# Layer norm, linear attention and a mixture of experts in one kernel: where the last batch's routed operand is made, and the order of the routing steps

## The reference

```python
xn = _layernorm(x)
s = _L0_attn_ref(xn, ...)             # 16 heads of 8 channels, softmax over 1024 keys, plus a depthwise conv of v
def _experts_mlp(x, g, W1, b1, W2, b2):
    xn = _rmsnorm(x, g)               # x * rsqrt(mean(x*x) + eps) * g
    h = gelu(einsum('btc,ech->bteh', xn, W1) + b1)      # 128 -> 512
    return einsum('bteh,ehc->btec', h, W2) + b2         # 512 -> 128
h_s = _experts_mlp(u, g_shared, ...).sum(axis=-2)       # 2 shared experts, all tokens
scores = sigmoid(u @ centroids)                         # 8 routed experts
gpk, i_topk = top_k(scores, 2)
gk = gpk / scores.sum(axis=-1, keepdims=True)
h_r = sum over the 2 picks of gk * routed expert of that pick
return u + h_s + h_r                                    # u is xn
x = x + s * silu(...)
```

## Time and profile before

| | us |
|---|---|
| device time, median of 3 runs | 1215.17 (1215.11 to 1217.58) |
| the profiled execution | 1215.84 |
| its span | 1213.8 |
| PE busy in the span | 1150.0 (95%) |
| DVE busy | 831.8 (69%) |
| ACT busy | 750.3 (62%) |
| POOL busy | 392.2 (32%) |

### The profile page before, as it was taken

The page is one execution under the profiler, slowest core; times in us unless marked ns, Lnnn a source line. Parts: engine busy times, 40 slices in busy tenths (PEclk is TensorE's granted clock), DMA queues, the critical chain, the costliest instruction groups (busy, mean ns, idle before and its releaser), DMA issues.

```text
span 1213.8 us, 18390 instructions
## 1 busy us (share of the span) xinstructions
PE 1150.0 (95%) x6564; PEld 727.3 (60%) x6564; DVE 831.8 (69%) x1562; ACT 750.3 (62%) x1385; POOL 392.2 (32%) x436
## 2 busy tenths in 40 slices
PE   4899949979998999999999999999999999999996
PEld 3788839979985545555554555555455555545542
DVE  6642213235637888888889888888988888898870
ACT  4544416635546767666676666667666666766676
POOL 0055565020006543514324351432435043243000
PEclk8799979989999999999999999999999999999998
DMA  9011133555433212020211203021111202112000
GB/s 335 5 41 38 42 102 113 165 142 150 141 104 80 55 39 53 20 75 11 58 37 35 52 18 77 11 58 36 35 44 28 75 11 58 37 35 51 9 6 5
DMA packets 73866, 75.36 MB, mean 62 GB/s; under 512 B 25248, under 2 KB 58912, under 8 KB 73264
## 3 DMA queue, kind: packets, MB, share of 16 engines
q1 hardware_dynamic: 69680, 65.80, 19.7%
q0 software_dynamic: 4096, 8.40, 2.4%
HBM read 30.06 MB, written 18.35 MB: 40 GB/s over the span
## 4 chain that ended last, share of the span: by engine, by line
PE 63%; DVE 6%; issue 1%; ACT 0%; POOLq 0%; POOL 0%; DVEq 0%; ACTq 0%
PE ps L1377 22%; PE ps L1389 20%; PE ps L1034 18%; DVE neg_half L1101 4%; PE ps L1055 1%; DVE acc L1448 1%; PE ps L1063 1%; PE ps L1060 0%; DVE pre L1130 0%; PE ps L1048 0%; DVE pv_sb L1453 0%; ACT prob L1417 0%; DVE attn L1144 0%; DVE r_sum L1139 0%; POOLq L779 0%
## 5 line engine op out<-in xcount | busy, mean ns | idle before, releaser
L1101 DVE TENSOR_REDUCE neg_half<-ps 128x1 f32<-128x512 f32 x1024 | 647.2, 684 | 177.9 <-PE ps L1034 169.9
L1417 ACT ACTIVATE prob<-ps 128x512 f32<-128x512 f32 x1024 | 545.1, 598 | 210.9 <-PE ps L1377 191.5
L1377 PE MATMUL ps<-q_raw,k_mask 128*128 128x512 f32 x1024 | 431.7, 427 | 4.1 <-ACTq L1410 3.9
L1034 PE MATMUL ps<-k_raw,q_mask 128*128 128x512 f32 x1024 | 412.8, 403 | 9.1 <-DMA q_mask<-raw 6.3
L1377 PEld LDWEIGHTS ps<-q_raw,k_mask 128*128 128x128 f32 x1024 | 191.7, 188 | 231.5 <-ACT prob L1417 160.4
L1389 PE MATMUL ps<-prob,v_st 128*32 128x512 f32 x2048 | 272.8, 604 | 2.5 <-issue 1.2
L1034 PEld LDWEIGHTS ps<-k_raw,q_mask 128*128 128x128 f32 x1024 | 193.8, 189 | 50.6 <-DVE neg_half L1101 14.5
L594 ACT ACTIVATE hidden<-ps,w 128x512 f32<-128x512 f32 x92 | 62.9, 688 | 83.6 <-PE ps L503 77.2
L1331 POOL TENSOR_TENSOR result<-attn,acc 128x256 f32<-128x256 f32 x16 | 11.8, 734 | 293.6 <-DVE attn L1144 157.8
L520 PEld LDWEIGHTS ps<-w,hidden 128*128 128x128 f32 x736 | 95.3, 193 | 6.2
L520 PE MATMUL ps<-w,hidden 128*128 128x128 f32 x736 | 97.5, 276 | 0.0
(11 more groups left out here) (145 smaller groups left out, 1011.7 us busy)
## 6 DMA issues: line engine op xcount, KB each, us to landing
w<-in_w SPq DMA_DIRECT2D x23, 322.0 KB, 3.9
k_mask<-k_raw SPq DMA_DIRECT2D x64, 96.0 KB
slots<-zero SPq DMA_DIRECT2D x4, 1472.0 KB, 11.0
w_raw<-in_w SPq DMA_DIRECT2D x23, 256.0 KB, 2.8
x_tok<-slots SPq DMA_DIRECT2D x23, 256.0 KB, 3.2
answers<-y_tok SPq DMA_DIRECT2D x23, 256.0 KB, 2.3
k_raw<-raw SPq DMA_DIRECT2D x16, 256.0 KB
q_mask<-raw SPq DMA_DIRECT2D x64, 64.0 KB
```

The lines of the kernel that those rows point to most:

```text
L1034: nc.tensor.matmul(max_bank(par, k, lone_bank)[:, :], q_mask[par][:, j, qt * P:(qt + 1) * P], k_raw[par][:, kh * CH:(kh + 1) * CH], start= ...
L1101: nc.vector.tensor_reduce(out=neg_half[par][:, qt, j, kh:kh + 1], in_=max_bank(par, k, lone_bank)[:, :], axis=AX.X, op=ALU.max, negate=True)\
L1377: nc.tensor.matmul(score_bank(n, par, s)[:, :], k_mask[par][:, j, kt * P:(kt + 1) * P], q_raw[par][:, qh * CH:(qh + 1) * CH], start=True, ...
L1417: nc.scalar.activation(prob[s // J % 2][:, j, :], score_bank(n, par, s)[:, :], ACT.Exp, scale=SCALE)\
```

## The change

The change has these parts:

- The last batch's `xr_all` is no longer transposed in the prologue. PE does it in `rest()`, after the up step 6 of shared unit 1, into `aux`; ACT rounds it into `xrh` after the gelu of step 7, DVE makes `xrl` at the start of unit 2. `gains` moves to a place that lives through both stages.
- In the prologue DVE calls `low_parts` of the batch before after the batch's `acc`, not between its statistics. The last batch has none.
- The gate products wait for each half of `xnT` on its own, not for both.
- `count` comes after the up step 3, not 4.
- The list `expert` is made behind the slots, and `placed` is incremented after each pick. POOL sends all tiles of pick 0, then all of pick 1, waiting after each four.
- The convolution's batches go in units 3, 4, 5, 7, not 2, 3, 5, 7. The first value product waits for `rest_ok`.

```diff
@@ prologue, DVE
                 own_steps.did(last)
-                if b > 0:
-                    low_parts(b - 1)
                 own_steps.settle(apart=True)
...
                     nc.vector.tensor_scalar(acc[:, b * QT + t, :], xb[:, t, :], mv[:, t, 0:1], rstd[:, t:t + 1],
                                             ALU.subtract, ALU.mult).then_inc(xn_ok, 1)
+                if b > 0:
+                    low_parts(b - 1)
...
-            low_parts(B - 1)
@@ prologue, ACT
-                for h in range(2):
+                for h in range(2 if b < B - 1 else 0):
                     act.wait_ge(xrT_full, 2 * b + h + 1)
...
+            act.wait_ge(xr_ok, TILES)
             act.wait_ge(logit_ok, 1)
@@ prologue, PE
-                for h in range(2):
+                for h in range(2 if b < B - 1 else 0):
                     pe.wait_ge(xr_ok, QT * b + 4 * (h + 1))
...
-                pe.wait_ge(xnT_out, 2 * b + 2)
                 for t in range(b * BT, (b + 1) * BT):
+                    if t % BT % CT == 0:
+                        pe.wait_ge(xnT_out, 2 * b + t % BT // CT + 1)
@@ experts
-    COUNT_AT, CONV_AT, TURN_AT = 4, 0, 5
-    CONV_IN = {2: 0, 3: 1, 5: 2, 7: 3}
+    COUNT_AT, CONV_AT, TURN_AT, REST_AT = 3, 0, 5, 6
+    CONV_IN = {3: 0, 4: 1, 5: 2, 7: 3}
@@ experts, POOL
-            pool.wait_ge(placed, 1)
-            for t in range(TILES):
-                for k in range(TOPK):
+            for k in range(TOPK):
+                pool.wait_ge(placed, k + 1)
+                for t in range(TILES):
                     nc.gpsimd.indirect_dma_start(out=io["slots"], ...)
                       .then_inc(moved_in[k], 16)
-                if t % 2 == 1:
-                    for k in range(TOPK):
+                    if t % 4 == 3:
                         pool.wait_ge(moved_in[k], 16 * (t + 1))
@@ experts, PE
+            def rest():
+
+                pe.wait_ge(placed, 1)
+                for h in range(2):
+                    for t in range(CT):
+                        last = nc.tensor.transpose(aux[h][:, t * P:(t + 1) * P],
+                                                   ffn["xr_all"][:, TILES - BT + h * CT + t, :], ident[:, :])
+                    last.then_inc(rest_full, 1)
...
                 if b == 0:
-                    pe.wait_ge(placed, 1)
+                    pe.wait_ge(rest_ok, 2)
...
+                    if u == 1 and q == REST_AT:
+                        rest()
@@ experts, ACT
+                if u == 1 and q == REST_AT + 1:
+                    for h in range(2):
+                        act.wait_ge(rest_full, h + 1)
+                        nc.scalar.activation(ffn["xrh"][:, rest_of(h)], aux[h][:, :], ACT.Copy,
+                                             scale=ffn["gains"][:, 0:1]).then_inc(rest_hi, 1)
@@ experts, DVE
-            step(nc.vector.tensor_tensor(past[:, :, :], ...))
-            step(nc.vector.reduce_sum(which[:, :], past[:, :, :], axis=AX.X))
-            step(nc.vector.tensor_scalar(keep["expert"][:, :], which[:, :], float(ER - 1), None, ALU.min))
-            dve.sem_inc(listed, 1)
...
                 step(nc.vector.tensor_copy(keep["slot"][:, k, :], slot_f[k][:, :]))
-            dve.sem_inc(placed, 1)
+                dve.sem_inc(placed, 1)
+            step(nc.vector.tensor_tensor(past[:, :, :], ...))
+            step(nc.vector.reduce_sum(which[:, :], past[:, :, :], axis=AX.X))
+            step(nc.vector.tensor_scalar(keep["expert"][:, :], which[:, :], float(ER - 1), None, ALU.min))
+            dve.sem_inc(listed, 1)
...
             for u, q in steps():
+                if (u, q) == (2, 0):
+                    for h in range(2):
+                        dve.wait_ge(rest_hi, h + 1)
+                        nc.vector.scalar_tensor_tensor(ffn["xrl"][:, rest_of(h)], aux[h][:, :], ffn["gains"][:, 0:1],
+                                                       ffn["xrh"][:, rest_of(h)].bitcast(F32),
+                                                       ALU.mult, ALU.subtract).then_inc(rest_ok, 1)
```

More of the change, by code:

```diff
@@ L102, in prologue @@
         w1_in = sb("w1_in", [P, ES, HID])
-        gains = sb("gains", [P, 2])
+        gains = ffn["gains"]
         cent = sb("cent", [P, ER])
@@ L376, in experts @@
         v_full = sem("f_v_full")
+        rest_full = sem("f_rest_full")
+        rest_hi = sem("f_rest_hi")
+        rest_ok = sem("f_rest_ok")
         v_ok = sem("f_v_ok")
@@ L396, in steps, with rest_of @@
             return [(u, q) for u in range(UNITS) for q in range(of(u))]
+        def rest_of(h):
+            return slice(NTOK - T + h * CH, NTOK - T + (h + 1) * CH)
         def next_at(u, q):
@@ L677, in _ @@
                 step(nc.vector.tensor_copy(keep["slot"][:, k, :], slot_f[k][:, :]))
-            dve.sem_inc(placed, 1)
+                dve.sem_inc(placed, 1)
+            step(nc.vector.tensor_tensor(past[:, :, :],
+                                         ffn["places"][:, :].rearrange("p (k a) -> p k a", a=1)
+                                         .broadcast_to([P, ROUTED, ER]),
+                                         blocks_upto[:, :].rearrange("p (a e) -> p a e", a=1)
+                                         .broadcast_to([P, ROUTED, ER]),
+                                         ALU.is_ge))
+            step(nc.vector.reduce_sum(which[:, :], past[:, :, :], axis=AX.X))
+            step(nc.vector.tensor_scalar(keep["expert"][:, :], which[:, :], float(ER - 1), None, ALU.min))
+            dve.sem_inc(listed, 1)
             step(nc.vector.reduce_sum(total[:, :], score[:, :, :], axis=AX.X))
@@ L1501, in run @@
             small = {"rank": [TILES, ER], "before": [P], "ones": [P], "steps": [BT], "places": [ROUTED],
-                     "th": [TILES, ER], "w2s": [ES, W2_ROW], "wv": [C], "cols": [5], "gain_r": [1],
+                     "th": [TILES, ER], "w2s": [ES, W2_ROW], "wv": [C], "cols": [5], "gain_r": [1], "gains": [2],
                      "xr_all": [TILES, C]}
```

## The result

The kernel after the change takes 1200.9 us (median of 4 runs, 1199.52 to 1201.72) beside 1215.57 of the kernel before (4 runs): a ratio of 0.9865, interval 0.9849 to 0.9881. The profiled execution took 1201.72, with a span of 1199.7.

The account below looks back on a forecast made before the run. Prologue, DVE's routing and POOL's scatters were taken to bound the first 176 us. Terms 4.28 + 1.44 + 0.8 + 1.09 + 1.13 - 0.2 = 8.5 took 1215.84 to 1207.3, forecast as a 1206.7 median; range 1202.5 to 1211.0.

Parts of the forecast that it names:

- the term of the scatters' waits: POOL's scatters: one wait for each four instead of two, possibly worth 0 to 1.5 us, taken as 0.
- The prologue's pipeline: Prologue: with `low_parts` moved, DVE and ACT wait less, so batch 3's normed tiles start 4.28 us earlier.
- The last batch: End of the prologue: without the last transposes, copies and `low_parts`, tiles to tanh shortens by 1.44 us, table load hidden.
- The half clock: Last batch's gate products on PE: granted clock taken as 0.50, so they cost 3.42 us.
- Routing: DVE's chain before the first scatter: earlier `count` 0.8, list 1.09 and second pick 1.13 us out of the way.
- DVE beside the scatters: Start of POOL's scatters: DVE's list, second pick and gates now run beside them, costed as a 0.2 us delay.
- `rest()`: Shared units: eight transposes moved there cost PE about 1.03 us, all hidden under the scatters.
- The bound: First 176 us: prologue, DVE's routing, then POOL's scatters set the end; PE's shared units finish 17.43 us earlier.
- the prologue was not held elsewhere: Rival, chance 0.13: something else, such as banks freed later, holds the prologue; most of 4.28 us is lost, giving 1210.9.
- the fours of one pick land no later: Rival, chance 0.05: four scatters of one pick land later; 0.57 us more per wait eats the gain, up to 1217.6.
- the chain was the end: Rival, chance 0.03, claimed the opposite: PE's shared units set the end, giving 1215.2 to 1216.7.
- The rival of the full clock: Chance 0.16: last batch's gate products run at 2.4 GHz and `count` is never late, 1.57 + 0.27 us more, giving 1204.9.

## Why the prediction was wrong, and where it was right

**The step that failed** is the term of the scatters' waits: "a wait that has been satisfied costs next to nothing; 15 of them can be worth 0 to 1.5 us (0.1 each). I take 0." The waits of the trace say otherwise: 0.48 each as a rule, 7.8 in all (0.52 on average), and 8.09 by the stretch. With 8.1 for that term, and the sum's 0.2 for DVE gone, the same sum is 16.8 (8.5 + 0.2 + 8.1). The two misses of the prologue below (1.28 and 0.69) take it to 14.8, and the 0.7 left to the span's 14.1 lies within what the stages behind came out longer (0.08 - 0.07 + 0.9).

The reading error is worth more than the number. I priced the second wait by POOL's memset, which came 1.37 behind its last scatter through several waits. That row is right: the memset had four waits in front of it before (1.37) and three after (1.31), so a wait more cost it 0.06. But the question was what they cost in front of an indirect DMA, and that too stood in the rows: 31.0 / 15 = 2.07 behind each four. The 0.7 between 2.07 and 1.37, 15 times over 10 us, was left unexplained. After the change 1.53 stands against 1.31, so 0.22 of the gap is there with a single wait too.

**The prologue's pipeline** (4.28) was right in all three of its steps: the tiles of batches 1 to 3 started 6.32, 13.59 and 20.87 after the first batch's, forecast 6.23, 13.90 and 21.19. Against the 25.47 of before that is 4.60. **The last batch** (1.44) did not come: from its tiles to the tanh it took 8.38, before 8.27, forecast 6.83. "Its table load for the tanh lies there" was wrong: the change puts a second wait in front of the tanh, and the load came after the products, 1.28 lost, until a wait was moved (then 7.04). The products themselves were 0.16 longer than forecast. From the first tiles to the tanh it took 29.25, forecast 28.0, before 33.74. Besides, this execution's input came 0.69 later (first statistics at 7.69, not 7.00), which is no part of the change. The forecast start of the first scatter, 54.3, also takes off the 0.2 that lies behind it; by the terms it is 54.1. It came at 55.92, and the prologue is nearly all of the difference. The Trainium skill, "ScalarE: Activation LUTs", section "What ACT_TABLE_LOAD costs", states some 1283 ns for the load, and a drain of about 1380 ns with each switch; the trace agrees on the first (1.28) and shows no drain between the load and the tanh, which starts at 41.65, 0.01 behind the load's end.

**The half clock** of the gate products was chosen rightly: 3.58 at a granted clock of 0.50 (1.2 GHz), against 3.42 before.

**Routing** came out at 3.12 for 3.02. DVE's wait for `count` fell from 2.13 to 1.22, forecast about 1.1.

**DVE beside the scatters** (0.2) was nothing that can be seen in the sum: the first scatter took 1.30 (1.22 before), with the list's first step beginning at 56.95 beside it, and the first four took 5.09 from start to end, before 5.50. The Trainium skill, "SBUF — State Buffer", section "SBUF: two separate sides", states that some DVE operations lock GpSimd out while it writes the descriptors of a POOL DMA; the trace shows no such lock-out for the length of the list and the second pick (2.2). But the slow scatters do have DVE beside them. Behind the first one, 23 of after's scatters overlap a DVE step of 512 or more columns, and 12 of these took over 1.0 us, up to 1.68 beside the step at 90.01; of the 40 others none took over 0.97. The kernel before shows the same (9 of 24 up to 1.44, the others at most 0.97), so this is no part of the change.

**`rest()`** cost 1.04 on PE, forecast 1.03. DVE stood 8.1 before its part of it, for ACT's copies; nothing on PE waited for that.

**The bound** was right, and the rivals stand as they were weighed: the prologue was not held elsewhere, the fours of one pick land no later, and the chain was the end, since PE still waited 5.1 for the block. The rival of the full clock didn't come. None of them had the waits in it; the range took in 1.5 for a term whose row allowed ten.

## What to carry to other kernels

Price a wait by a row in which the same kind of instruction stands behind it, and explain every gap between two rows that should show the same thing before a term is set to nothing. Where it can be had, put one wait in front of an instruction, not two: count on one semaphore, or put the wait that is met anyway behind something else. And before a pause is taken out of one engine's stream, look at which others go on in it: pauses behind four or six scatters paid here, behind eight all of the gain was lost, and with no pause at all the kernel was 50 us slower than the kernel before.

## What the runs showed of the hardware

A second wait in a row costs an indirect DMA of POOL 0.48 us (2.01 against 1.53) even where it was met long before; in front of a memset one wait more cost 0.06 (1.37 against 1.31). On ACT two waits in a row put the 1.28 us of a table load behind the event, one let it run before (behind the products in after; beside them with the wait moved, and in the kernel before). Why a second wait does this, no run shows.

A stream of scatters without pauses stopped ACT for 23.9 and 25.3 us although what it computes on was there, at a DMA share of only 0.15. With pauses of 1.53 behind fours nothing of this shows: PE is busy for 100.11 of the 102.38 us.

The first one apart, a scatter of POOL took longer than usual only beside a wide step of DVE: in after over 1.0 us in 12 of 23 cases beside steps of 512 or more columns, at most 0.97 in the 40 others. Why not in all 23, no row shows.
